# Wide-head attention: the keys from three fp32r products of split context and weights, in place of one fp32 product

## What is computed

```python
xn = _layernorm(x, ln_gamma, ln_beta)               # x is itself normalised before
q = (xn @ w_q).reshape(B, SQ, NUM_HEADS, DIM_HEAD)  # 16 heads of 64
kv = context @ w_kv
k, v = jnp.split(kv, 2, axis=-1)
scores = jnp.einsum('bqhd,bkhd->bhqk', q * SCALE, k)
attn = jax.nn.softmax(scores, axis=-1)
out = jnp.einsum('bhqk,bkhd->bqhd', attn, v).reshape(B, SQ, INNER)
return (out @ w_out + b_out) * jnp.tanh(gate[0])
```

## Time and profile before

| | |
|---|---|
| median of 3 runs | 1094.25 us (1086.43 to 1097.5) |
| the profiled execution, its own time | 1095.44 us |
| its span | 1093.7 us |
| granted TensorE clock, mean over the span | 0.851 of full |
| TensorE, VectorE, ScalarE, GpSimd busy | 816.1, 678.3, 473.1, 410.0 us |
| first and last start of a keys product | 153.9 and 315.3 us |
| last addition of the stage's projection begins | 349.8 us |

### The profile page before, as it was taken

How to read it: one execution, slowest core, us unless ns; L and a number is a source line. 1 busy time by engine, 2 the same in 40 slices (tenths; PEclk the granted TensorE clock), 3 DMA queues, 4 the chain that set the end, 5 groups by cost and what they waited for, 6 DMA issues and landing times.

```text
span 1093.7 us, 23671 instructions
## 1 busy us (share of the span) xinstructions
PE 816.1 (75%) x8135; PEld 682.8 (62%) x8135; DVE 678.3 (62%) x1649; ACT 473.1 (43%) x928; POOL 410.0 (37%) x496
## 2 busy tenths in 40 slices
PE   6998989999997899955777557477667189958105
PEld 3766877888885799744666547477667056643005
DVE  3886567777776777671333245544444659977794
ACT  4774435454452444323444423144333046634753
POOL 5672311110101611115766630267765256610610
PEclk9998889999999699986979875699888559977557
DMA  6200000000000000023444548545443300000001
GB/s 194 67 0 2 1 1 3 2 2 0 0 2 2 6 19 19 20 86 90 125 129 130 130 137 261 170 104 153 131 125 101 85 1 1 1 1 1 0 0 38
DMA packets 77120, 64.02 MB, mean 59 GB/s; under 512 B 9649, under 2 KB 66546, under 8 KB 77042
## 3 DMA queue, kind: packets, MB, share of 16 engines
q1 hardware_dynamic: 70428, 50.60, 16.1%
q0 software_dynamic: 5888, 12.07, 4.5%
q10 hardware_dynamic: 726, 0.33, 0.1%
HBM read 49.08 MB, written 13.89 MB: 58 GB/s over the span
## 4 chain that ended last, share of the span: by engine, by line
PE 59%; DVE 17%; issue 9%; ACT 5%; another core or an unknown queue 4%; DMA 2%; SPq 1%; POOL 1%; DVEq 1%; ACTq 1%; POOLq 0%
PE psum L1140 6%; PE psum L1837 4%; PE psum L1811 3%; PE psum L1813 3%; PE psum L738 3%; PE psum L643 3%; PE psum L680 3%; PE psum L658 3%; PE psum L1812 2%; PE psum L373 2%; PE psum L2108 2%; PE psum L347 2%; PE psum L317 2%; PE psum L1109 2%
## 5 line engine op out<-in xcount | busy, mean ns | idle before, releaser
L1811 PE MATMUL psum<-E_XH,E_WH 128*128 128x256 f32 x230 | 76.6, 333 | 77.4 <-DVE E_XL L1967 54.3
L1936 POOL DMA_INDIRECT y_scratch<-E_y,route_place_of x92 | 97.8, 1064 | 72.9 <-DVE E_y L1989 25.7
L1926 POOL DMA_INDIRECT E_rows<-rows_scratch,route_token_of x92 | 96.9, 1053 | 68.5 <-DVE route_token_of L1609 36.7
L1811 PEld LDWEIGHTS psum<-E_XH,E_WH 128*128 128x128 f32 x230 | 50.4, 219 | 84.0 <-DVE E_XL L1967 58.4
L1397 DVE SCALAR_TENSOR_TENSOR X<-psum,E_gates,X 128x128 f32<-128x128 f32 x256 | 71.8, 345 | 26.2 <-PE psum L1140 26.2
L1837 PE MATMUL psum<-E_w,E_h 128*128 128x128 f32 x644 | 85.6, 286 | 2.7 <-issue 2.7
L1837 PEld LDWEIGHTS psum<-E_w,E_h 128*128 128x128 f32 x644 | 81.3, 203 | 4.0 <-issue 3.9
L493 POOL TENSOR_TENSOR A_kexp<-A_kT,hmask 128x512 f32<-128x512 f32 x64 | 66.4, 1058 | 32.5 <-ACT A_kT L414 32.5
L1140 PEld LDWEIGHTS psum<-E_w,E_h 128*128 128x128 f32 x512 | 67.8, 194 | 11.5 <-ACT E_h L1226 6.0
L1140 PE MATMUL psum<-E_w,E_h 128*128 128x128 f32 x512 | 68.7, 277 | 4.7 <-ACT E_h L1226 4.0
L1813 PE MATMUL psum<-E_XH,E_WL 128*128 128x256 f32 x230 | 71.6, 311 | 0.0
(11 more groups left out here) (315 smaller groups left out, 2194.3 us busy)
## 6 DMA issues: line engine op xcount, KB each, us to landing
E_w<-in_L_xattn_W SPq DMA_DIRECT2D x46, 256.0 KB
E_w<-w_scratch SPq DMA_DIRECT2D x23, 384.0 KB
E_w<-w_scratch SPq DMA_DIRECT2D x23, 192.0 KB
E_back<-y_scratch SPq DMA_DIRECT2D x16, 256.0 KB, 4.9
w_scratch<-E_stage SPq DMA_DIRECT2D x8, 384.0 KB, 3.0
rows_scratch<-xn SPq DMA_DIRECT2D x8, 256.0 KB, 2.3
E_w<-in_L_ffn_routed_w SPq DMA_DIRECT2D x28, 64.0 KB, 1.9
w_scratch<-E_stage SPq DMA_DIRECT2D x8, 192.0 KB, 3.5
```

The source lines that it names most:

```text
L1811: pe.matmul(out, WH[:, p, ws], XH[:, p, :], start=True, stop=False)
L1926: pool.indirect_dma_start(out=xg[:, i % 4, b, :], out_offset=None, in_=rows[:, :], in_offset=bass.IndirectOffsetOnAxis(ap=disp.token_of[:, ...
L1936: pool.indirect_dma_start(out=yrows[:, :], in_=y[:, i % 3, b, :], in_offset=None, out_offset=bass.IndirectOffsetOnAxis(ap=disp.place_of[:, ...
```

## The change

The keys are computed as three products instead of one, as in the experts. Context c and weights w are each split in a high part, rounded to fp32r, and a low part, the rest in fp32r; the product is cH wH + cL wH + cH wL, added up in PSUM.

- Once, at the start: ScalarE copies `w["k"]` (128 x 1024) to `wkH`, ahead of all its work for the layer. VectorE waits for it and makes `wkL` by subtraction, ahead of the first statistics. TensorE waits for `w_split` before the first keys.
- Per tile: GpSimd copies the tile's 128 columns of context to `kcH` and subtracts to make `kcL`, one tile ahead, between the outer `rstd` and `ctx1`. Both have two buffers. TensorE waits for `kc_split` before the keys of the tile.
- TensorE: 24 matmuls per tile in place of 8.

```diff
--- before.py
+++ after.py
@@ -593,6 +593,8 @@
         xnT = sb("xnT", [P, 2, P])
         qT = sb("qT", [P, 2, HP, P])
         ctx1 = sb("ctx1", [P, 2, P])
+        kcH, kcL = (sb(name, [P, 2, P], F32R) for name in ("kcH", "kcL"))
+        wkH, wkL = (sb(name, [P, H * dh], F32R) for name in ("wkH", "wkL"))
         kT = sb("kT", [P, 2, HP, 2, S])
         v = sb("v", [P, 2, 2, HP, dh])
         prob = sb("prob", [P, 2, H, S])
@@ -622,6 +624,8 @@
     q_ps, q_ready = signal("q_in_psum", 2 * NT), signal("q_ready", 2 * NT)
     k_ps, k_ready = signal("k_in_psum", 2 * NT), signal("k_ready", 2 * NT)
     v_ps, v_ready, ctx1_ready = signal("v_in_psum", 2 * NT), signal("v_ready", 2 * NT), signal("ctx1_ready", NT)
+    kc_high, kc_split = signal("key_context_high", NT), signal("key_context_split", NT)
+    w_high, w_split = signal("w_high_ready", 1), signal("w_split", 1)
     scores_ready, mx_ready, sub_ready = signal("scores_ready", NT), signal("mx_ready", NT), signal("sub_ready", NT)
     prob_ready, probT_ps, probT_ready = signal("prob_ready", NT), signal("probT_in_psum", 2 * NT), signal("probT_ready", 2 * NT)
     o_ps, sm_ready, rc_ready, on_ready = signal("o_in_psum", NT), signal("sm_ready", NT), signal("rc_ready", NT), signal("on_ready", NT)
@@ -634,14 +638,18 @@
         m.begin(pe, start)
         pe.wait_ge(*m.dispatch.owner_ready(1))
 
+        pe.wait_ge(*w_split(1))
+
         def keys(t, p):
+            pe.wait_ge(*kc_split(t + 1))
             for j in range(2):
                 if past(t, 1):
                     pe.wait_ge(*q_ready(2 * t - 1 + j))
                 for c in range(4):
-                    cc = 4 * j + c
-                    mm = pe.matmul((J1, J0)[j][:, c * P:(c + 1) * P], w["k"][:, cc * P:(cc + 1) * P],
-                                   columns(m.ctxT, t, P), start=True, stop=True)
+                    ws, out = slice((4 * j + c) * P, (4 * j + c + 1) * P), (J1, J0)[j][:, c * P:(c + 1) * P]
+                    pe.matmul(out, wkH[:, ws], kcH[:, p, :], start=True, stop=False)
+                    pe.matmul(out, wkH[:, ws], kcL[:, p, :], start=False, stop=False)
+                    mm = pe.matmul(out, wkL[:, ws], kcH[:, p, :], start=False, stop=True)
                 mm.then_inc(k_ps.sem, 1)
 
         def values(t, p):
@@ -763,6 +771,7 @@
 
     def scalar(act):
         m.begin(act, start)
+        act.activation(wkH[:, :], w["k"], ACT.Copy).then_inc(w_high.sem, 1)
 
         def step(n, p):
             q = 1 - p
@@ -815,6 +824,15 @@
     def gpsimd(pool):
         m.begin(pool, start)
 
+        def key_context(t, p):
+            if past(t, 2):
+                pool.wait_ge(*k_ps(2 * t - 2))
+                apart(pool, m)
+            pool.tensor_copy(kcH[:, p, :], columns(m.ctxT, t, P)).then_inc(kc_high.sem, 1)
+            pool.wait_ge(*kc_high(t + 1))
+            apart(pool, m)
+            pool.tensor_tensor(kcL[:, p, :], columns(m.ctxT, t, P), kcH[:, p, :], ALU.subtract).then_inc(kc_split.sem, 1)
+
         def context(t, p):
             if past(t, 2):
                 pool.wait_ge(*v_ps(2 * t - 2))
@@ -825,9 +843,12 @@
                 inner.rstd(pool, n, p, xn_ready)
             if live(n + 1):
                 outer.rstd(pool, n + 1, 1 - p, x1_ready)
+            if live(n + 1):
+                key_context(n + 1, 1 - p)
             if live(n - 1):
                 context(n - 1, 1 - p)
 
+        key_context(0, 0)
         outer.rstd(pool, 0, 0, x1_ready)
         raw = m.weight_buffers["E3"][0]
         pool.memset(raw[:, :, :, :].rearrange("p a k f -> p (a k f)"), 0.0).then_inc(m.raw_zeroed[0], 1)
@@ -889,6 +910,8 @@
                     dve.wait_ge(*v_ps(2 * t + b + 1))
                     dve.tensor_copy(v[:, p, b].rearrange("p c d -> p (c d)"), (J1, J0)[b]).then_inc(v_ready.sem, 1)
 
+        dve.wait_ge(*w_high(1))
+        dve.tensor_tensor(wkL[:, :], w["k"], wkH[:, :], ALU.subtract).then_inc(w_split.sem, 1)
         outer.stats(dve, tile_of(m.X, 0), 0, 0)
         pipeline(dve, step, LO, HI, END)
```

## The result

| | before | after |
|---|---|---|
| median of 4 runs each | 1094.0 us | 1117.16 us (1112.77 to 1119.05) |
| ratio, 95% interval | | 1.0209 (1.016 to 1.0258) |
| the profiled execution, its own time | 1095.44 us | 1112.77 us |
| its span, granted clock | 1093.7 us, 0.851 | 1111.0 us, 0.847 |
| full step of the stage | 11.71 us | 12.55 us |

The change makes the kernel slower by about 23 us; 1114 us was predicted. The interval of the ratio lies clear of 1, though not of a difference of 2%. Ratios leave out executions in a slower state of the chip. Each experiment is compared with runs of before on the same chip in the same sitting, whose median was 1094.2 us beside e1 to e4, 1095.0 beside e5 to e7 and 1089.9, on another chip, beside e8 to e10.

A forecast was written before the change was run, and what follows sets the result against it. TensorE was taken to bound the stage; 13.4 + 5.5 + 1.7 - 0.9 = +19.7 us on 1095.4 gave 1115.1, so 1114, the profiled execution being 1.2 above the median. Range 1103 to 1127, its own 1110 to 1121.

The forecast's parts named there:

- Which engine binds, and that no other takes its place: Wide-head attention: TensorE busy 30.00 of 30 us mid-stage and still binding after; GpSimd's added work costs 0.
- The keys, +0.89 us a tile, +13.4: Keys of tiles 1 to 15: 24 records at one weight load each against 16, +13.4 us (-5.3 to +16.4).
- Counting passes, three for four: Keys: three passes for fp32's four would make them a quarter cheaper, -0.45 us a tile; weighed, not taken.
- The start, +5.5: Stage start: first keys wait for the weight split and run longer at low clock, +5.5 us (5.0 to 6.0).
- The clock at the start, +1.7: First queries and perhaps second keys: clock rises later behind fp32r keys, +1.7 us (0 to 4.3).
- The stall that hides, -0.9: TensorE's 0.91 us wait before 181.44, behind VectorE's copy of v, can hide behind longer keys: -0.9 us.
- Loads hidden: Rival, 4%: in the keys columns count, not loads; keys fall 0.35 us a tile, 1094.5 us, starts 0.06 apart.
- More array cycles for narrow fp32r: Rival, 3%: 128 fp32r columns take as long as the fp32 product; keys +3.6 us a tile, about 1155 us.
- Clock low in every step: Rival, 5%: clock low during each tile's keys, 5.1 instead of 2.7 us, 34 us more, about 1148 us.
- Partly absorbed: Rival, 8%: gaps of the last steps and queued VectorE work take up to 10 us of the delay; 1104 to 1106.

The follow-up runs named there:

- e1: Changed kernel without the third key product (low weights times high context), so 16 records per tile; 1108.18 us, ratio 1.0136.
- e4: Changed kernel with each key product cut in two of 64 moving columns, 48 records per tile; 1207.58 us in one run.
- e5: e3 with only tile 0's keys made by the one fp32 product, waiting for no split; 1107.7 us, ratio 1.01.
- e7: Changed kernel with VectorE doing tile 0's statistics before the subtraction for the low weights; 1112.6 us in one run.
- e8: e6 with fp32 keys for the first pair, first context splits behind the first rstd, GpSimd's memset at the stage's end; 1091.66 us, ratio 0.9999.
- e10: The kernel of e5 a second time; 1110.5 us in one run.
- e2: Changed kernel with keys made by one fp32 product again, both splits and their waits kept; 1101.41 us, ratio 1.0084.
- e6: Changed kernel with keys made for two tiles at once (256 moving columns, 12 records a tile), weights split early as in e3; 1093.69 us, ratio 0.9991.
- e3: Changed kernel with the key weights split by GpSimd ahead of the layer, instead of by ScalarE and VectorE; 1113.45 us, ratio 1.0185.
- e9: The kernel of e2 a second time; 1102.75 us in one run.

## Why the prediction was right

**Which engine binds, and that no other takes its place.** Right: 30.00 us of 30 before and after, clock 1.00, and GpSimd at 4.6 to 5.3 of 30 us, where under 6 was announced. e2 puts the price of its two instructions at zero.

**The keys, +0.89 us a tile, +13.4.** Right in kind and size: 384 records over three lines, 24 a step, and a step of 12.55 us where 12.6 was announced, so +0.84 a tile and 15 x 0.84 = +12.6. The keys themselves grew by 2.80 - 1.88 = 0.92; 0.08 came back at their start. e5, where the start is that of before, bears the term out with a stage 13.05 us longer. The term stood on a reading of 46-column products. The runs confirm it from three sides: 64, 128 and 256 columns stand 0.111, 0.113 and 0.119 apart (e4, after, e6), two fp32r products cost one fp32 product (e1), and a change of the columns hardly matters while a change of the loads does. Counting passes, three for four, pointed to the wrong sign: the Trainium skill, FP8 and Floating Point Precision, section TensorE Precision Notes, gives four passes for true fp32, but the trace shows two records with a load each for it, against three. How many passes a record holds, no trace here shows.

**The start, +5.5.** Right: "to transpose" grew by 10.85 - 5.05 = 5.8 us. First keys were announced for 157.7; they began at 158.77, 1.0 of it because the stage was reached later. The text priced both ends, the keys and the norm behind VectorE's queue, and took the keys; e7 shows that the keys bind.

**The clock at the start, +1.7.** The size is about right, the reason was half of it. From the first transpose to the last the stage grew by 178.22 - 163.38 = 14.84 us; 12.6 are keys, so 2.2 are left, 1.6 of them in the queries (3.36 against 1.78) and 0.4 in the second keys (2.94 us from first to last start, 2.59 at the full clock). The prediction put it down to fp32r keys behind which "a gap of 0.9 us comes". e3 bears this out, where the pause is gone and the clock low. But e2 and e9 have fp32 keys and a low clock too; what they keep is the 4.3 us pause. In these traces either went with a low clock, and e5 and e10, which have neither, had the full one. That the term came out near its size is in part luck: how long the clock stays low differed by about 1 us between e2 and e9, the same kernel twice.

**The stall that hides, -0.9.** Wrong. It stood in the step that "can hide behind longer keys", but it is still there, with the same length (timeline of TensorE in after, against the earlier trace rows):

```profile
192.90 0.30 PE L676 MATMUL psum<-ident,A_xn 128*128 128x128 f32 x1 [0.91 <-DVE A_v L911]
```

By the order of a step the values (L658) stand behind the keys (L643), and the copy of v waits for the values. So longer keys move both the waiter and what it waits for. A longer piece of TensorE's own work hides only a chain on another engine that began ahead of it.

**The sum.** 12.6 + 5.8 + 2.2 = 20.6 us on the stage, where 13.4 + 5.5 + 1.7 - 0.9 = 19.7 was predicted: the terms were off by -0.8, +0.3, +0.5 and +0.9, together 0.9. The profiled time grew by 17.3 us: 20.6 in the stage and 1.0 ahead of it, less 4.3 behind it (746.1 against 750.4 us from the end of the stage to the end of the span). The medians grew by 23.2. The prediction had no term for the time behind the stage, so that its 19.7 lies between the two is luck. By the bounds that it names, its own range is 1112 to 1120 and not 1110 to 1121; this changes nothing here.

**The rivals.** Loads hidden: no, starts stand at 0.11. More array cycles for narrow fp32r: no, else 0.22. Clock low in every step: not here, but in e4. Partly absorbed: the stage lost all of it.

## What to carry to other kernels

Before a product is replaced by several cheaper ones, count the records with a weight load in the trace and take the distance between starts; with 4-byte types and up to 128 moving columns that distance was one load each, 0.11 us, and neither the length of a record nor the number of passes tells it. Split products pay only when a load feeds enough columns, here 256, and operands that must be prepared should be prepared on an idle engine before the stage, with the first tile left in the old form. A gain of 3 to 4 us in one stage is less than the time behind that stage varies by from one trace to the next, so judge such a change by the stage first, and do not expect the median to show it.

## What the runs showed of the hardware

- TensorE's clock fell in e4_half_width with matmul records open for all of the time, to 0.77 to 0.92 over windows of 30 us, where the keys were 48 records of 64 columns with a load each; with 24 records of 128 columns it stayed at 1.00.
- The same work with the same short waits (0.85, 0.78 and 0.78 us in the experts) ran at clock 1.00 in the execution of before and at 0.70 in that of e8_pair_keys_fp32_first.
- An operation of VectorE that takes 0.35 us took 2.02 beside a memset of GpSimd. It ran from 159.92 in after, the memset from 159.84; in e7, where the memset was over, the same operation took 0.34 us (VectorE and GpSimd in after, then VectorE in e7_stats_first):

```profile
159.92 2.02 DVE L154 TENSOR_SCALAR A_x<-X,A_A_outer_meanvar,A_A_outer_rstd 128x128 f32<-128x128 f32 x1 [0.68 <-POOL A_A_outer_rstd L150]
```

```profile
159.84 2.02 POOL L854 MEMSET E_raw<- 128x2304 f32 x1
```

```profile
158.34 0.34 DVE L154 TENSOR_SCALAR A_x<-X,A_A_outer_meanvar,A_A_outer_rstd 128x128 f32<-128x128 f32 x1
```

In after it lies beside the first keys and costs nothing. In e1, e2 and e9, whose first keys are shorter, VectorE's chain with this operation in it ends last, and the first transpose waits for it (1.33 us in e2); so a part of their "to transpose" of 9.80 us is this collision.
